# VectorE writes the low part of the normalised attention output before a step's sums, quantisation parts and weight low parts

## What is computed

```python
x = L0_attn_hidden_states                      # (8, 512, 512)
xn = _layernorm(x)
qkv = xn @ Wqkv_w.T + Wqkv_b                   # 16 query, 8 key, 4 x 256 value columns
p1, p2 = softmax(q1 @ k1.T * scale, causal), softmax(q2 @ k2.T * scale, causal)
o = (p1 - lam * p2) @ v                        # 8 heads, 256 wide
o = o * rsqrt(mean(o * o) + EPS) * subln_w * (1.0 - LAMBDA_INIT)
s = o.reshape(B, S, H * D) @ out_w.T + out_b
g = _silu(quant_dequant_mxfp4(xn) @ quant_dequant_mxfp4(weight).T + bias)
x = x + s * g
```

## Time and profile before

| | |
|---|---|
| median of 3 runs | 1578.58 us (1578.43 to 1583.26) |
| profiled execution, its own time | 1581.34 us |
| its span | 1579.5 us |
| PE busy | 1479.2 us (94% of the span) |
| DVE busy | 1131.8 us (72%) |
| ACT busy | 889.4 us (56%) |
| POOL busy | 882.6 us (56%) |

### The profile page before, as it was taken

The page is one execution under the profiler, slowest core; times in us unless marked ns, Lnnn a source line. Parts: engine busy times, 40 slices in busy tenths (PEclk is TensorE's granted clock), DMA queues, the critical chain, the costliest instruction groups (busy, mean ns, idle before and its releaser), DMA issues.

```text
span 1579.5 us, 27518 instructions
## 1 busy us (share of the span) xinstructions
PE 1479.2 (94%) x8966; PEld 863.8 (55%) x8982; DVE 1131.8 (72%) x2654; ACT 889.4 (56%) x2474; POOL 882.6 (56%) x1587
## 2 busy tenths in 40 slices
PE   5877789999999999999999999999999999999988
PEld 2444345556555556455565565555655565646654
DVE  5888887667775777757877678766777578775771
ACT  4666775367633667247753577436773477534660
POOL 2566546565565655655565655656556555555553
PEclk9989899999999999999999999999999999999999
DMA  8246453334423453235433335334432444423433
GB/s 266 58 90 138 90 93 65 93 82 78 81 63 87 84 93 75 50 97 78 95 67 88 79 73 95 65 94 81 90 69 55 94 87 91 71 61 76 71 76 74
DMA packets 382496, 134.76 MB, mean 85 GB/s; under 512 B 361872, under 2 KB 365968, under 8 KB 382352
## 3 DMA queue, kind: packets, MB, share of 16 engines
q1 hardware_dynamic: 382352, 132.99, 40.6%
HBM read 35.93 MB, written 8.39 MB: 28 GB/s over the span
## 4 chain that ended last, share of the span: by engine, by line
PE 28%; DVE 27%; ACT 15%; POOL 14%; issue 9%; DMA 4%; SPq 1%; ACTq 0%; POOLq 0%; DVEq 0%
PE ps L544 8%; PE ps L545 8%; PE ps L546 8%; DVE ps L1011 6%; DVE qkv L976 5%; ACT pp L713 5%; DVE pp L1017 4%; ACT qkv L690 4%; DMA out_x<-res 2%; ACT on L735 2%; POOL qkv L1209 2%; ACT ph L722 2%; DVE aq L877 2%; POOL row L1239 2%; DVE ph L1023 1%
## 5 line engine op out<-in xcount | busy, mean ns | idle before, releaser
L1225 POOL TENSOR_TENSOR row<-row,small 128x1 f32<-128x1 f32 x256 | 147.0, 574 | 415.8 <-ACT pp L713 415.8
L722 ACT ACTIVATE ph<-pp,small 128x128 f16<-128x128 f32 (+3 forms) x256 | 142.7, 557 | 318.6 <-DVE pp L1017 318.3
L544 PE MATMUL ps<-xT,wqkv 128*128 128x512 f16 x768 | 296.3, 386 | 25.5 <-DVE qkv L976 9.8
L713 ACT ACTIVATE pp<-ps,row 128x384 f32<-128x384 f32 (+3 forms) x512 | 268.3, 524 | 61.9 <-DVE row L1011 56.4
L545 PE MATMUL ps<-xT,wqkv 128*128 128x512 f16 x768 | 296.4, 386 | 0.0
L546 PE MATMUL ps<-xT,wqkv 128*128 128x512 f16 x768 | 295.7, 385 | 0.0
L1011 DVE CUSTOM_DVE_ANT_0 ps<-ps,mask,ssc 128x384 f32<-128x384 f32 (+3 forms) x512 | 261.9, 552 | 10.3 <-PE ps L613 9.5
L976 DVE SCALAR_TENSOR_TENSOR qkv<-ps,bsc,qkv 128x512 f16<-128x512 f32 x192 | 143.5, 750 | 115.7 <-ACT qkv L690 115.6
L1029 DVE SCALAR_TENSOR_TENSOR on<-ps,row,on 128x256 f16<-128x256 f32 x256 | 123.7, 483 | 119.5 <-ACT on L735 116.7
L544 PE MATMUL ps<-qkv,pT 128*128 128x256 f16 x640 | 176.1, 275 | 30.4 <-DMA pT<-ph 21.6
L1023 DVE SCALAR_TENSOR_TENSOR ph<-pp,small,ph 128x128 f16<-128x128 f32 (+3 forms) x256 | 157.5, 615 | 61.3 <-ACT ph L722 60.5
(11 more groups left out here) (132 smaller groups left out, 2977.2 us busy)
## 6 DMA issues: line engine op xcount, KB each, us to landing
xres<-in_x SPq DMA_DIRECT2D x32, 256.0 KB, 2.9
out_x<-res SPq DMA_DIRECT2D x32, 256.0 KB, 2.3
wqkv<-in_wqkv SPq DMA_DIRECT2D x15, 512.0 KB, 6.6
xin<-in_x SPq DMA_DIRECT2D x7, 1024.0 KB, 5.9
vbias<-in_bv SPq DMA_DIRECT2D x32, 128.0 KB, 3.2
pT<-ph SPq DMA_TRANSPOSE x256, 2.7
wout<-in_ow SPq DMA_DIRECT2D x8, 512.0 KB, 4.2
heads<-on SPq DMA_TRANSPOSE x128, 3.2
```

The costliest lines, as they stand in the source:

```text
L544: mm(out, ah, bh, start=start and j == 0, stop=False)
L713: run(out, sc_ps[u][:, m, 0:w], ACT.Exp, bias=ebias[:, u, m:m + 1], scale=-1.0, accum_out=psum_l[:, n % 6, m:m + 1]).then_inc(exp_done, 1)
L722: run(ph[:, n % PH, 0:w], pp[:, 1 + u, 0:w], ACT.Copy, scale=sigma).then_inc(ph_hi, 1)
```

## The change

In each step VectorE now writes the low part of unit n-1 (with its wait for `on_hi`, and in three steps the copy `take` of the small product's result, which must precede it) directly after `p_lo` and `gating`, ahead of `squares` or `o_squares`, of the "maxima" slot, of `w_low` and of `o_low`. Nothing is added or taken out, and the instructions of PE, ACT, POOL and SP stand in the same order as before.

```diff
                 for f in PLAN[n - 1] if n else ():
                     if f.kind == "ffn":
                         gating(f)
+                if n - 1 in NORM_STEP:
+                    dve.wait_ge(on_hi, n)
+                    take(junk[(n - 1) % 2], 4)
+                if n:
+                    normalised_lo(n - 1)
                 if SUM_STEP.get(n) == 5:
                     o_squares()
                 elif n in SUM_STEP:
                     squares(SUM_STEP[n])
...
                 for p in range(OP):
                     if OUT_SPLIT[p] == n - 1:
                         o_low(p)
-                if n - 1 in NORM_STEP:
-                    dve.wait_ge(on_hi, n)
-                    take(junk[(n - 1) % 2], 4)
-                if n:
-                    normalised_lo(n - 1)
```

## The result

| | before | after |
|---|---|---|
| median | 1579.33 us (4 runs, 1578.43 to 1583.26) | 1590.30 us (4 runs, 1586.16 to 1591.08) |
| ratio | | 1.0063, 95% interval 1.0045 to 1.0081 |
| profiled execution | 1581.34 us | 1590.54 us |
| its span | 1579.5 us | 1588.7 us |
| PE busy | 1479.2 us | 1480.0 us |

The change costs about 10 us, 0.63%. Forecast were 8.3 us, and 1586.9 us (1579.5 to 1592.0). The busy times are those of before; all of the loss is waiting.

What follows compares the result with a forecast made beforehand. The prediction took batch 0 to be bound by its chain of fills on VectorE, POOL and ScalarE, not PE's waits. Its terms, 7.4 - 2.1 + 3.0 = +8.3 us, moved the median from 1578.6 to 1586.9 us, range 1579.5 to 1592.

Steps and rivals of the forecast that it cites:

- Term 1: Batch 0: VectorE waits for ScalarE's high part with its moved work behind it, so fills come 7.4 us late.
- the prediction's formula: A fill is late by the high part's end plus 0.04 us, minus the time VectorE is free behind `p_lo`.
- nine others: Nine smaller steps of batch 0, from step 1 to step 28, together 3.3 us late, 1.0 of it in step 7.
- Term 2: Steps 2, 4, 8, 11: `w_low` no longer delays POOL's L1237; fills 0.53 us earlier each, 2.1 us in all.
- Term 3: Batch 0: VectorE and POOL exclude each other in new places, in steps 6, 23, 30, 31 and 4, 27, 28, 29; 3.0 us late.
- The four dead heats: Steps 6, 23, 30, 31: weight's low part and POOL's L1225 start together; 0.42 us late each, 1.7 us in all.
- The clock: Rival, chance 0.12: longer PE waits in batch 0 lower the granted clock by another 0.02, 4 us more, 1591 us.
- Batches 1 to 7: Fourteen places behind batch 0, each 0.4 us late on VectorE by the formula, costed at nothing.
- the cover by PE's long `out` fill: Later batches: PE's 48 matmuls, some 10 us, hide the fourteen delays; without it they cost 5.6 us.
- a longer time behind batch 0: Sign of a wrong prediction: the batches behind batch 0 lengthen, where the rest of the span should stay as before.
- The end of batch 0 has no slack: Opposes the rival, chance 0.25, that batch 0's tail has slack, so only terms up to step 20 count: +4.1, 1582.7 us.
- PE's waits for L1029 were not the bound: Opposes the rival, chance 0.06, that PE's waits for L1029, not the fills, bound batch 0: -5.4, 1573.2 us.

Runs made afterwards that it cites:

- three steps: New order in steps 14, 16 and 31 of batch 0 alone, all else as in the kernel before: median 1583.65 us, ratio 1.0021.
- step 20 alone: New order in step 20 of batch 0 only, all else as in the kernel before: median 1580.66 us, ratio 1.0006.
- batch 0 alone: New order in all steps of batch 0, old order in batches 1 to 7, against the kernel before: median 1588.74 us, ratio 1.0044.

## Why the prediction was right

**Term 1, VectorE waits with its work behind it: right.** Forecast and measured, in us: step 14 1.6 and 1.46, step 16 1.0 and 0.85, step 31 0.84 and 0.84, step 20 0.65 and 0.63 by itself. Of the smaller ones step 1 gave 0.29, step 3 0.25, step 10 0.40, step 13 0.35, steps 23 and 24 0.24 each; step 7 gave 0.8 where 1.0 stood. The runs with three steps and with step 20 alone show for these four that each is caused by its own step and that they add. Step 18 gave 0.7 us, 0.45 for the wait and 0.25 for the `combine` behind it, and seems to stand in no term: its wait comes to 0.6 by the prediction's formula (182.06 + 0.04 - 181.49), and nine others make up the 3.3 us without it. In the profile that the forecast was worked out from, PE's slow fill stood there and covered it.

**Term 2, the relief: right.** -2.1 forecast for the fills of four steps, -2.08 in the kernel with these steps alone.

**Term 3, the exclusion elsewhere: half right.** The `combine` behind steps 4, 27, 28 and 29 was forecast 0.32 late each beside VectorE's own wait. Steps 27 to 29 came to 1.55 us with the waits' 0.6, so 0.3 each. The four dead heats, 1.7 us in the sum, cost nothing: steps 6 and 30 moved by 0.05 and 0.06 us, and steps 23 and 31 by no more than their waits. POOL's rows at step 30, then VectorE's:

```profile
251.58 0.55 POOL L1225 TENSOR_TENSOR row<-row,small 128x1 f32<-128x1 f32 x1 [1.00 <-ACT pp L713]
252.23 0.84 POOL L1227 TENSOR_SCALAR row<-row,small 128x1 f32<-128x1 f32 x1
```

```profile
251.59 1.28 DVE L923 SCALAR_TENSOR_TENSOR wout<-wout,small 128x1024 f16<-128x1024 f32 x1
252.78 0.74 DVE L983 SCALAR_TENSOR_TENSOR v<-vbias,vscale,ps 128x512 f32<-128x512 f32 x1
```

POOL started 0.01 us first and was recorded for 0.55 us. VectorE nevertheless began and ended its 1.28 us as if alone, and it is the next POOL instruction that was stretched, from 0.34 to 0.84. The same stands at steps 6, 23 and 31. 0.01 us is little to tell an order by, but the kernel before shows it with more: in steps 14, 18 and 31 POOL's L1239 had begun 0.39, 0.48 and 0.25 us before the weight's low part, and both took what they take alone (0.55 and 1.27 to 1.28 us). So the records suggest that a one-column POOL instruction holds what the two share for far less than its record.

**The clock: a rival that came true in one place.** It stood at 0.12, with 4 us for a granted clock lower by 0.02 from 60 to 257 us. That did not come: it was 0.93 before and 0.94 after. What came was 1.6 us at step 20, in the profile after and in that of batch 0 alone, a fall in a place where the chain felt it. Together with the 0.7 us of step 18 it makes up for the four dead heats that cost nothing, so the stretch of batch 0 came out at the forecast partly by luck: against 193.7 to 193.9 us, which three profiles of the old order without a fall at step 20 show, the 202.08 us after are 8.2 to 8.4 us longer. Without the 1.6 it would be some 6.7, and without step 18 too, some 6.0.

**Batches 1 to 7: the step that failed.** "I cost the fourteen places at nothing" was wrong by 3.6 us (1.7 to 5.7), which is less than the 5.6 that were named if the cover by PE's long `out` fill was gone. The prediction gave a longer time behind batch 0 as a sign that it is wrong, and by that sign this part of it is. The median of 1590.30 us lay in the range nevertheless, near its upper end, since the range had room for the clock. VectorE's delay in step 1 is as forecast (0.42), that in step 3 is 0.25 where 0.4 was taken. Alone, step 1's is given back in all batches but one; step 3's stays on VectorE's times, yet not in the timed runs. Together the timed runs show a loss, and the profiles show the path of half of it at most.

**The rivals.** The end of batch 0 has no slack: step 31's 0.84 us arrived in full. PE's waits for L1029 were not the bound: they fell by 6.1 us for no gain, and those for the transposes grew by 7.4.

## What to carry to other kernels

Putting a short instruction first because the busiest engine waits for it can cost more than it gives, if it has to wait itself and has work behind it that needs nothing. Compare two times at each place: when what it waits for is ready, and when its engine is free. Only where the first is earlier, or where the work that it overtakes delays the very thing it waits for (here POOL's L1237), does it belong in front; and then look at what else delays that thing, which was worth four times as much (7 us beside 1.8).

## What the runs showed of the hardware

Two engines exclude each other by what they use and not by their records: a VectorE instruction with two tensors from SBUF stretched POOL's L1237 from 0.19 to 1.17 us and its L1227 from 0.34 to 0.84, while a POOL instruction of 128x1 elements, started 0.01 us ahead in four places and 0.25 to 0.48 us ahead in three, did not delay VectorE at all. The Trainium skill, page "SBUF — State Buffer", section "Who interferes with whom", says that a VectorE instruction with two inputs in SBUF contends with a GpSimd instruction that reads SBUF, that the order of issue decides who is blocked, and, of VectorE's two-port modes, that whoever issues first has the shared pair for the whole instruction. The trace agrees where VectorE is first, and where POOL's instruction is 512 wide (2.29 us for a `w_low` beside two of them); for a POOL instruction of one column the measurement decides against it.

One and the same program was granted 1.2 GHz in different places from one execution to the next: in the fill at 177 us for all of its twelve matmuls, for seven or eight of them, or for none, and in the scores of step 20 in one of six profiles in which the program is the same up to there (1.67 us). The Trainium skill, page "TensorE: Matmul & The Clock Gate", section "What's actually happening", says that what opens and closes the clock gate runs free and does not start anew with a kernel. That the places differ from one execution to the next agrees with this. Behind batch 0 one such stretch, with a late transpose ahead of it, moved VectorE by up to 2.6 us. So differences between two profiles of under 3 us need their place named, or many timed runs.
